# Value tiles of the next context ahead of the query and output projections, and denominators ahead of numerators, in a fused decoder kernel

## The reference

```python
q = softmax(heads(x @ Wq.T + bq), axis=-1)          # 16 heads of 16
k = softmax(heads(y @ Wk.T + bk), axis=-1)
v = heads(y @ Wv.T + bv)
k_cumsum = sum(k, axis=-2)
D_inv = 1.0 / sum(q * k_cumsum, axis=-1)
kv  = einsum('bhnd,bhne->bhde', k, v)
out = q + einsum('bhnd,bhde->bhne', q, kv) * D_inv
x   = layernorm(x + out @ Wp.T + bp)
```

## Time and profile before

| | us |
|---|---|
| median of 3 runs | 1829.25 |
| lowest, highest | 1828.51, 1831.0 |
| profiled execution, its time | 1831.61 |
| profiled execution, span from first to last instruction | 1829.6 |
| TensorE matmul busy | 1733.8 (95%) |
| TensorE weight load busy | 1516.8 (83%) |
| VectorE busy | 1222.6 (67%) |
| ScalarE busy | 987.0 (54%) |
| mean granted TensorE clock | 0.982 |

### The profile page before, as it was taken

The page is one execution under the profiler, slowest core; times in us unless marked ns, Lnnn a source line. Parts: engine busy times, 40 slices in busy tenths (PEclk is TensorE's granted clock), DMA queues, the critical chain, the costliest instruction groups (busy, mean ns, idle before and its releaser), DMA issues.

```text
span 1829.6 us, 27298 instructions
## 1 busy us (share of the span) xinstructions
PE 1733.8 (95%) x10508; PEld 1516.8 (83%) x10508; DVE 1222.6 (67%) x1897; ACT 987.0 (54%) x1516; POOL 18.6 (1%) x42
## 2 busy tenths in 40 slices
PE   2599999999999998998999999999999999999997
PEld 1388888778888787887899889998899989999896
DVE  6989999999999856888444444444454544445446
ACT  4789998998999782444533333233333333333323
POOL 1000000000000000000000000000000000000000
PEclk9699999999999998999999999999999999999999
DMA  7301110011011002111111011110001001120001
GB/s 185 58 1 30 24 58 18 18 32 61 12 24 40 1 29 89 45 55 45 56 35 36 1 35 35 34 34 0 34 34 34 24 10 34 34 75 0 1 1 41
DMA packets 37967, 64.79 MB, mean 35 GB/s; under 512 B 3287, under 2 KB 22013, under 8 KB 36861
## 3 DMA queue, kind: packets, MB, share of 16 engines
q1 hardware_dynamic: 34620, 55.47, 9.4%
q0 software_dynamic: 3264, 8.19, 3.0%
HBM read 59.99 MB, written 3.67 MB: 35 GB/s over the span
## 4 chain that ended last, share of the span: by engine, by line
PE 84%; DVE 7%; ACT 6%; DMA 2%; issue 1%; SPq 0%; ACTq 0%; POOL 0%; DVEq 0%; POOLq 0%
PE fbank L1986 33%; PE fbank L2008 17%; PE pair L882 8%; PE pair L867 7%; PE pair L842 7%; PE pair L852 5%; PE proj L1480 2%; PE qbanks L1516 1%; PE pair L832 1%; PE abanks L1516 1%; PE kvp L1568 1%; ACT kf L659 1%; ACT kfh L661 1%; DMA wckl<-in_w_ck 1%; ACT kf L657 1%
## 5 line engine op out<-in xcount | busy, mean ns | idle before, releaser
L1808 DVE TENSOR_TENSOR hf<-sil,fbank 128x512 f32<-128x512 f32 (+1 forms) x256 | 158.8, 620 | 479.4 <-PE fbank L1986 403.6
L1913 ACT ACTIVATE sil<-fbank 128x512 f32<-128x512 f32 (+1 forms) x256 | 139.2, 544 | 615.3 <-PE fbank L1986 615.2
L1986 PE MATMUL fbank<-xh,wh 128*128 128x512 f32 (+1 forms) x1024 | 289.8, 364 | 1.2 <-ACT sil L1913 1.2
L1986 PE MATMUL fbank<-xh,wl 128*128 128x512 f32 (+1 forms) x1024 | 288.9, 363 | 0.0
L1986 PE MATMUL fbank<-xl,wh 128*128 128x512 f32 (+1 forms) x1024 | 288.7, 363 | 0.0
L2008 PE MATMUL fbank<-wl,hh 128*128 128x256 f32 x896 | 250.3, 279 | 0.0
L2008 PE MATMUL fbank<-wh,hh 128*128 128x256 f32 x896 | 250.2, 279 | 0.0
L2008 PE MATMUL fbank<-wh,hl 128*128 128x256 f32 x896 | 250.1, 279 | 0.0
L1986 PEld LDWEIGHTS fbank<-xl,wh 128*128 128x128 f32 x1024 | 184.4, 189 | 30.7
L1986 PEld LDWEIGHTS fbank<-xh,wl 128*128 128x128 f32 x1024 | 184.4, 189 | 30.3
L1986 PEld LDWEIGHTS fbank<-xh,wh 128*128 128x128 f32 x1024 | 180.7, 189 | 27.8 <-ACT sil L1913 1.6
(11 more groups left out here) (240 smaller groups left out, 3111.2 us busy)
## 6 DMA issues: line engine op xcount, KB each, us to landing
raw<-in_w_gate SPq DMA_DIRECT2D x16, 512.0 KB, 3.8
raw<-in_w_up SPq DMA_DIRECT2D x16, 512.0 KB, 4.7
raw<-in_w_down SPq DMA_DIRECT2D x16, 512.0 KB, 5.8
raw<-in_w_ck SPq DMA_DIRECT2D x4, 1024.0 KB, 7.2
raw<-in_w_cv SPq DMA_DIRECT2D x4, 1024.0 KB, 7.4
wcvl<-in_w_cv POOLq DMA_DIRECT2D x6, 512.0 KB, 5.9
raw<-in_ctx_t SPq DMA_DIRECT2D x4, 750.0 KB, 6.1
ct<-in_ctx_t SPq DMA_DIRECT2D x4, 750.0 KB, 4.9
```

What stands on the lines that cost most here:

```text
L1808: dve.tensor_tensor(hf[i][:, 0:w], sil[i][:, 0:w], banks(e, t, f)[1][:, 0:w], ALU.mult).then_inc(hf_ready, 1)
L1913: act.activation(sil[f % 2][:, 0:w], banks(e, t, f)[0][:, 0:w], ACT.Silu).then_inc(sil_ready, 1)
L1986: ins = pe.matmul(banks(e, t, f)[k][:, 0:w], m[h][:, o:o + P], a[:, b, columns(c)], start=i == 0, stop=i == 3 * CB - 1)
```

## The change

Two edits. In the first, `project` is cut in two: `project_values(s)` has the two value tiles with their waits, `project_rest(s)` all that follows. In stages with i = 0 or 3 both are called where `project` was. In stages with i = 1 or 2 `project_values(n + 1)` is called at the head of the stage, ahead of the query projection, of the output projection and of `turn_x2`. In the second, `by_heads` issues all denominators, signals `den_done`, and then issues all numerators and signals `num_done`. VectorE's reciprocal waits for `den_done` instead of `num_done`, and its products in `attend` wait for `num_done` too. No instruction is added or removed on any engine but for one wait on VectorE in each of four places.

```diff
             def denominators(c):
 
-                dve.wait_ge(num_done, c + 1)
+                dve.wait_ge(den_done, c + 1)
                 dve.reciprocal(drec[:], dens).then_inc(den_read, 1)
...
                 dve.wait_ge(den_read, c + 1)
+                dve.wait_ge(num_done, c + 1)
                 after(did(dve.tensor_tensor(heads(num[:]), head_banks(abanks), spread(drec), ALU.mult)))
...
+            def project_values(s):
                 pe.wait_ge(ctl_ready, s + 1)
                 if s:
 
@@ -1489,18 +1490,20 @@
                 else:
                     pe.wait_ge(wkvl_ready, 1)
                 for t in range(2):
-                    ins = tile(STILES + 1 + t, t, slice(C, 2 * C))
+                    ins = context_tile(s, STILES + 1 + t, t, slice(C, 2 * C))
                 ins.then_inc(v01_done, 1)
+
+            def project_rest(s):
                 if s:
 
                     pe.wait_ge(v2_ready, s)
                     pe.wait_ge(arg_ready, s)
-                tile(STILES, 2, slice(C, 2 * C))
+                context_tile(s, STILES, 2, slice(C, 2 * C))
...
             def by_heads(c):
 
+                def query(i, b):
+                    return qt[c % 2][:, b, i * T:(i + 1) * T]
+
                 for i in range(G):
-                    o = (c * G + i) % (2 * G)
                     for b in range(CB):
-                        qb = qt[c % 2][:, b, i * T:(i + 1) * T]
-                        pe.matmul(abanks[0:T, i // 2, (i % 2) * C + b * P:(i % 2) * C + (b + 1) * P], qb,
-                                  kvbd[:, o, b, :], start=True, stop=True)
-                        ins = pe.matmul(dens[:, i * H + b * (H // CB):i * H + (b + 1) * (H // CB)], qb,
-                                        kcm[:, o, b, :], start=True, stop=True)
+                        ins = pe.matmul(dens[:, i * H + b * (H // CB):i * H + (b + 1) * (H // CB)], query(i, b),
+                                        kcm[:, (c * G + i) % (2 * G), b, :], start=True, stop=True)
+                ins.then_inc(den_done, 1)
+                for i in range(G):
+                    for b in range(CB):
+                        ins = pe.matmul(abanks[0:T, i // 2, (i % 2) * C + b * P:(i % 2) * C + (b + 1) * P], query(i, b),
+                                        kvbd[:, (c * G + i) % (2 * G), b, :], start=True, stop=True)
                 ins.then_inc(num_done, 1)
...
             for n in range(B):
                 i, c1, c2 = stage(n)
+                if n + 1 < B and i in (1, 2):
+                    project_values(n + 1)
                 if i == 1 and c1 is not None:
                     pe.wait_ge(xt_ready, c1 + 1)
                     tokens_out(qbanks, xt, wq, 1, q_done)
...
                 if n + 1 < B:
-                    project(n + 1)
+                    if i in (0, 3):
+                        project_values(n + 1)
+                    project_rest(n + 1)
```

More of the change, by code:

```diff
@@ L1027, in attention_phase @@
         arg_ready, exp_ready, k_ready = sem("karg_ready"), sem("kexp_ready"), sem("k_ready")
-        bd_ready = sem("bd_ready")
+        bd_ready, den_done = sem("bd_ready"), sem("den_done")
         xin_in = [sem(f"xin_in{i}") for i in range(2)]
@@ L1473, in add_bias, with context_tile @@
                 return pe.matmul(out, onesr[:, 0:tokens], bias[:, j, :], start=False, stop=True)
[L1475 to L1483, removed]
+            def context_tile(s, out, t, cols):
+                n = 0
+                for a, w in ((cth, wkvh), (cth, wkvl), (ctl, wkvh)):
+                    for b in range(CB):
+                        ins = pe.matmul(proj[0:ST, out, :], a[s % 2][:, b, t * ST:(t + 1) * ST], w[:, b, cols],
+                                        start=n == 0, stop=n == 3 * CB - 1 and cols.start > 0)
+                        n += 1
+                return ins if cols.start else add_bias(proj[0:ST, out, :], 0, ST)
+            def project_values(s):
                 pe.wait_ge(ctl_ready, s + 1)
@@ L1497, in project @@
                     pe.wait_ge(arg_ready, s)
-                tile(STILES, 2, slice(C, 2 * C))
+                context_tile(s, STILES, 2, slice(C, 2 * C))
                 if s == 0:
                     pe.wait_ge(bias_ready, 1)
-                tile(2, 2, slice(0, C)).then_inc(v2_done, 1)
+                context_tile(s, 2, 2, slice(0, C)).then_inc(v2_done, 1)
                 for t in range(2):
-                    ins = tile(t, t, slice(0, C))
+                    ins = context_tile(s, t, t, slice(0, C))
                 ins.then_inc(proj_done, 1)
@@ L1574, in tensor @@
             pe.wait_ge(const_set, 4)
-            project(0)
+            project_values(0)
+            project_rest(0)
             pe.wait_ge(w_in, 32)
```

## The result

| | before | changed |
|---|---|---|
| median, us | 1829.82 (4 runs, 1828.51 to 1831.0) | 1820.68 (4 runs, 1819.54 to 1821.71) |
| profiled execution: time, span | 1831.61, 1829.6 | 1819.54, 1817.5 |
| mean granted clock | 0.982 | 0.985 |

What follows compares the result with a forecast made beforehand. TensorE, busy 1733.8 of 1829.6 us, was taken as the bound, so only its idle time could go. Terms 1.3 + 0.15 + 2.25 + 1.0 + 2.45 + 0.45 = 7.6 us off 1829.25 gave 1821.6, range 1818.5 to 1826.

Steps and rivals of the forecast that it cites:

- Stage 1: First query projection, at the lower clock: filled gap and earlier clock return gain 1.3 us, bounds 0.65 to 2.2.
- The formula: Stage 1: next context sum starts at t + 8.63 - (t - 712.5)/2, against 724.84 in the old order.
- t = 717.3: Stage 1: time the full clock returns, moved from 718.6 because gapless work begins 1.3 us earlier.
- Stage 4: Reciprocal of the denominators, which had waited 0.27 us: earlier denominators gain 0.15 us, bounds 0 to 0.65.
- Stages 5 and 6: Both projection gaps filled: keys done 2.45 us earlier, of which VectorE's key arguments let 2.25 through; bounds 1.0 to 2.5.
- Stages 9 and 10: Turn of x2 follows the output projection and moves only 1.0 us, so the gain is 1.0; bounds 0 to 2.5.
- the chain that the prediction named: Stages 9 and 10: behind x2's turn, ScalarE's copy, rounding and high context, then VectorE's low part, which waited 3.03 us.
- Stages 13 and 14: No further contexts to prepare, key arguments had waited for TensorE: the full 2.45 us comes through, bounds 1.0 to 2.5.
- The heads: Denominators first: nothing in stages 8 and 12, 0.45 us at the last attend (bounds 0 to 0.5).
- (a): Rival: only the first gap of each pair of stages comes through; sum 5.0 us, 1824.2; chance 0.2.
- (b): Rival: VectorE sets the pace, freed time returns as waits for keys; gain 1.75 us, 1827.5; chance 0.1.
- Rival (c): Clock falls in the four blocks of denominators, 3.4 us lost each; slower, 1835.3 us; chance 0.05.

Runs made afterwards that it cites:

- one value of i: Changed kernel with value tiles ahead only of the query projection (i = 1), ratio 0.9968, or only of the output projection (i = 2), ratio 0.9992.
- turn first: Changed kernel with the turn of x2 moved ahead of the output projection in stages 10 and 14; 1821.65 us, ratio 0.9949.
- denominators alone: Kernel before the change with denominators issued ahead of numerators, value tiles left where they were; ratio 0.9995.
- reciprocal first: Changed kernel with VectorE's reciprocal of the denominators ahead of the first norm's five small operations; 1825.95 us, one execution.
- routing in halves: Kernel with x2's turn first and last attend in pairs, with the first routing split around one product of the experts; 1818.56 us, ratio 0.9936.
- the same with the heads in pairs: Changed kernel with the turn of x2 ahead of the output projection and denominators and numerators in pairs as before; 1819.49 us, ratio 0.9942.

## Why the prediction was right

The time came at 1820.68 for 1821.6, inside the range and near the forecast. The gain is less near than the time: 9.1 us for 7.6. 0.6 of that 1.5 does not show in the time, since the forecast counts from a median of 1829.25 and the kernel before ran at 1829.82 beside the change. The mechanism, gaps on TensorE filled and the gain capped by the next engine in line, is what the runs show. By its own steps:

- **Stage 1,** forecast 1.3 (0.65 to 2.2), measured 2.46. This is the term that was mis-sized, past its upper bound. The formula held: the clock was down 6.8 us instead of 10.2, which on the scale of before is t = 708.4 + 6.8 = 715.2, and 715.2 + 8.63 - 2.7/2 = 722.48, a gain of 2.36. What failed is the choice of t = 717.3, made by moving the return by the length of the filled gap; the t of its upper bound, 715.5, was the near one. The return does not slide with the work; it came 3.4 us earlier at once, and in no profile anywhere between.
- **Stage 4,** forecast 0.15, measured 0.17 at the turn. The context sums themselves came 0.37 earlier, and 0.2 of that went into the wait for ScalarE's norm.
- **Stages 5 and 6,** forecast 2.25, measured 2.43. VectorE's key arguments now start without idle time behind the low weights, which is the cap that the forecast set; the cap itself had moved by some 0.15 more (the key arguments of stage 7 start 2.40 earlier than before, counted from the turn of stage 4, for the 2.25 of the forecast).
- **Stages 9 and 10,** forecast 1.0, measured 1.06. TensorE had 2.48 at context sums 10 and gave 1.42 back by context sums 11. The runs with one value of i and the one with the turn first show that it was the turn of x2, by the chain that the prediction named. One of its signs was off in size: the low part of context 12 was to wait about 3 us for ScalarE still, and waited 2.10 (807.60), 0.93 less than before.
- **Stages 13 and 14,** forecast 2.45, measured 2.50.
- **The heads,** nothing in stages 8 and 12, 0.45 at the end; measured 0 and 0.41. The cost on TensorE of denominators alone and numerators alone: in the last attend of the changed kernel they start at 863.38 and 864.97, and what follows at 866.71, 3.33 us in all, no more than pairs took (873.41 to 876.75, 3.34). That is 0.104 for each matmul of a pair; the 22 in 2.0 us that the forecast read from the earlier trace rows count also those that reach over an edge of the stretch.
- **Rivals (a) and (b)** are out, each with a run of its own. **Rival (c)** had a truth that the forecast weighed wrongly. Its argument against, a project before the denominators and wide matmuls behind, holds for three attends and not for the last one. In the eight profiles with single denominators ahead of the last numerators the clock fell there in four (denominators alone, only i = 1, turn first, reciprocal first), and in none of the five with that attend in pairs. By themselves four of eight against none of five could be chance; that such blocks can do it is shown by the run with three times as many, at four attends of four. A fall there lasted 3.4 us and cost 1.5 to 1.65, half of what the forecast priced, so that four of them, some 6.4 us, would have left the sign as it is. The changed kernel's two profiles have none. The forecast also passed over a stretch of its own trace that spoke against (c): the second piece of the routing is 16 narrow matmuls alone (16 columns each, 1.70 us to the next start) between long ones, and the clock held. It held there in all fourteen profiles:

```profile
906.92 1.85 PE L52 MATMUL kvp<-wrt,acc 128*128 128x16 f32 x16
908.62 0.37 PE L2008 MATMUL fbank<-wh,hh 128*128 128x256 f32 x1
```

```profile
906.00:908.00 2.00, 2.00 (x16) 1.83 (x14) 0.69 (x1) 0.36 (x1) 0.00 (x0) 1.00 0.00 0
908.00:910.00 2.00, 2.00 (x19) 2.00 (x19) 0.87 (x3) 1.17 (x3) 0.00 (x0) 1.00 0.00 0
```

- What the sum had no term for: the routing behind the part. Its block of narrow matmuls drew a fall of 6.8 us before and of 3.4 after, worth 1.65 us in favour of the change in the two profiles. That is luck as far as the forecast goes. The medians are 9.1 and 11.2 us apart in the two comparisons, on either side of 9.0 + 1.65; how often the other executions had the longer fall is not known.
- A slip in the forecast's rivals: (a) keeps stage 1 and three pairs but leaves out the 0.6 of the heads, which it does not touch, and (b) the 0.15 of stage 4; with them (a) is 5.6 us and 1823.6, (b) 1.9 and 1827.35. Neither changes the order of the rivals.

What stays open: why the clock fell at the last attend in some of the kernels with denominators first and not in others, beyond where it happened to stand in time; and why the kernel with the routing in halves has less of a gain in its median than by the ruler, whose rows come from one execution of each kernel. Where the clock fell in the unprofiled executions is not on record, but its mean in each is, and 0.001 of it is 3.6 us at the lower level: 0.984 to 0.986 in the nine executions of the changed kernel, 0.982 or 0.983 in all five with the turn first, 0.983 to 0.985 in the five of the same with the heads in pairs, 0.985 or 0.986 in the five with the routing in halves. That fits a further fall in nearly every execution of the kernel with the turn first and none in most of the last; these runs were on different chips, and the means do not say where the falls were.

## What to carry to other kernels

Where TensorE waits for another engine's copy of its own last result, put ahead of that wait any matmuls that must come anyway and whose inputs and banks are free; then follow each result that the moved block stood before, since the gain goes only as far as the next engine was waiting for TensorE, and where a side chain (here the turn of x2) hangs on the pushed block, move that chain's head forward too. Making a result early is worth nothing while the instruction that takes it stands behind other work in its queue. Keep narrow matmuls mixed with wide ones: gathered in blocks they cost nothing themselves, but they can take the clock down for what follows.

## What the runs showed of the hardware that I had not expected

- The granted clock came back, and fell, by jumps and not in proportion to the work moved: filling one gap of 1.0 us in stage 1 shortened the time at the lower level from 10.2 to 6.8 us, in ten profiles against four without an exception, worth some 2.5 us of the ruler.
- Behind 16 matmuls of 8 columns (1.6 us) that followed a turn and a stall of 0.57 us the clock went down for 3.4 us in four of eight profiles; with 48 of them it did so at all four attends, for 3.4 to 10.2 us (one profile). Behind 16 of 16 columns between long matmuls (1.7 us, the second piece of the routing) it stayed up in all fourteen profiles.
- The same 40 narrow matmuls of the routing drew a fall of 6.8 us (six profiles), of 3.4 us (seven), or, cut in two halves with 2.9 us of wide ones between, none (one).
- A gain of 2.2 us at the last context sums, seen in full in the timeline, was down to 0.1 to 0.2 us at the experts, since the fall then began 3.5 or 3.7 instead of 5.3 us after the routing's start and lasted twice as long. A change ahead of such a place can't be judged by the total alone.
